# Running the experts of a transformer layer over two halves of the tokens, with the first half's rows fetched and combined beside the second half's tiles

## The reference, cut to what matters

```python
x = x + ga * attention(layernorm(x) * (1 + ca) + sa)
h = layernorm(x) * (1 + cb) + sb
probs = softmax(h @ gate_w.T + gate_b)
_, topi = top_k(probs, 2)
for e in range(8):
    y = relu(h @ w1[e] + b1[e])
    y = relu(y @ w2[e] + b2[e])
    y = y @ w3[e] + b3[e]
    out = out + cw[..., e:e + 1] * y      # cw: the token's probability of expert e if e is one of its two, else 0
x = x + gb * out
```

## Time and profile before

| | before |
|---|---|
| median of 3 runs | 3917.32 us (3915.02 to 3924.01) |
| the profiled execution | 3909.84 us |
| its span, first to last instruction | 3908.2 us |
| TensorE busy | 3369.7 us (86% of the span) |
| VectorE busy | 2338.5 us (60%) |
| ScalarE busy | 1389.0 us (36%) |
| GpSimd busy | 1262.1 us (32%) |

### The profile page before, as it was taken

One profiled execution on the slowest core, in us unless ns is written; L12 is line 12 of the kernel. 1 busy time (PEld: TensorE's weight loads), 2 busy tenths in 40 slices (PEclk: granted clock), 3 DMA queues, 4 the chain that ended last, 5 costly groups with the idle time before them and its releaser, 6 DMA issues. The chain is left out here.

```text
span 3908.2 us, 163045 instructions
## 1 busy us (share of the span) xinstructions
PE 3369.7 (86%) x72200; PEld 2918.7 (75%) x72200; DVE 2338.5 (60%) x4708; ACT 1389.0 (36%) x1655; POOL 1262.1 (32%) x1486
## 2 busy tenths in 40 slices
PE   6964999999989999999799999989999999399900
PEld 4534888888878888888788888878888887388800
DVE  5853566677256667753566777346677771466633
ACT  1320233344612334354123334522233446255511
POOL 1004432322354332233443322344333211222266
PEclk8986999999989999999899999999999999699955
DMA  3764101000321110003111000131000000544444
GB/s 111 208 165 117 36 24 34 29 27 19 86 60 39 32 37 26 19 29 106 39 39 37 29 19 26 44 95 39 29 29 29 22 13 11 179 141 144 137 129 140
DMA packets 241113, 251.41 MB, mean 64 GB/s; under 512 B 102808, under 2 KB 183676, under 8 KB 240300
## 3 DMA queue, kind: packets, MB, share of 16 engines
q1 hardware_dynamic: 219308, 197.69, 17.3%
q0 software_dynamic: 21120, 43.42, 3.6%
HBM read 149.52 MB, written 90.23 MB: 61 GB/s over the span
## 5 line engine op out<-in xcount | busy, mean ns | idle before, releaser
L884 DVE TENSOR_TENSOR att_acc<-att_pm,att_acc 128x512 f32<-128x512 f32 x1920 | 1267.1, 687 | 539.0 <-PE att_pm L1002 267.8
L963 ACT ACTIVATE att_pt<-att_ps 128x1024 f32<-128x1024 f32 x560 | 573.3, 1024 | 1615.2 <-PE att_ps L994 1606.7
L991 PE MATMUL att_ps<-att_qx,table_x 68*128 68x64 f16 x8960 | 734.0, 195 | 9.1 <-issue 9.0
L994 PE MATMUL att_ps<-att_qz,table_z 128*128 128x64 f16 x8960 | 733.0, 195 | 6.0 <-issue 5.9
L966 ACT ACTIVATE att_pt<-att_ps 128x1024 f32<-128x1024 f32 x528 | 515.1, 1022 | 346.7 <-PE att_ps L1002 344.6
L994 PEld LDWEIGHTS att_ps<-att_qz,table_z 128*128 128x128 f16 x8960 | 624.2, 99 | 10.9 <-issue 10.8
L991 PEld LDWEIGHTS att_ps<-att_qx,table_x 68*128 68x128 f16 x8960 | 621.3, 99 | 7.3 <-issue 6.8
L1084 PE MATMUL att_po<-att_pt,att_vn 128*32 128x128 f32 x17408 | 597.4, 278 | 2.4 <-issue 2.2
L987 PE MATMUL att_ps<-att_qs,att_kn 113*128 113x64 f16 x8960 | 456.8, 195 | 81.6 <-DMA att_qs<-s_m 75.8
L987 PE MATMUL att_pm<-att_qs,att_kn 113*128 113x64 f16 x8672 | 444.1, 195 | 83.8 <-POOL att_qx L757 49.5
L1084 PEld LDWEIGHTS att_po<-att_pt,att_vn 128*32 128x32 f32 x17408 | 448.5, 110 | 87.4 <-issue 73.0
(11 more groups left out here) (210 smaller groups left out, 3925.1 us busy)
## 6 DMA issues: line engine op xcount, KB each, us to landing
att_qe<-s_q SPq DMA_DIRECT2D x256, 128.0 KB
moe_xs<-s_h SPq DMA_DIRECT2D x71, 256.0 KB, 3.2
s_y<-moe_y SPq DMA_DIRECT2D x71, 256.0 KB, 2.2
s_v<-prj_vx SPq DMA_DIRECT2D x32, 512.0 KB, 3.9
att_vn<-s_v SPq DMA_DIRECT2D x64, 256.0 KB, 3.2
att_qs<-s_q SPq DMA_DIRECT2D x128, 66.0 KB
prj_x<-in_x POOLq DMA_DIRECT2D x16, 512.0 KB, 4.6
att_kn<-s_k SPq DMA_DIRECT2D x128, 64.0 KB, 2.4
```

The costliest lines, as they stand in the source:

```text
L884: dve.tensor_tensor(held, got, held, ALU.max).then_inc(bank_done, 1)
L963: act.activation(pt[:, k % 2, :, t * 64:t * 64 + 64].rearrange("p h (x c) -> p x h c", x=2), ps[t][:, :, :].rearrange("p x (h c) -> p x h ...
L991: last = pe.matmul(groups[:, :, g], keep["table_x"][:, y:y + P], qx[0:G * D + G, s, x * (XQ // G) + g], start=False, stop=(g == XQ // G - ...
L994: last = pe.matmul(groups[:, :, g], keep["table_z"][:, y:y + P], qz[:, s, x * (XQ // G) + g], start=False, stop=(g == XQ // G - 1), skip_g ...
```

## The change

`HALVES` = 2: the first 32 blocks of 128 tokens (two sequences) are half 0, the others half 1. Each half has regions of its own in `s_h` (`PART` rows a half), a `taken` of its own, zeros of its own, and tables of its own of `NH` = 2 * 4096 / 256 + 7 = 39 tiles, so `NT` is 78. Results go to `s_y0` and `s_y1`. `tables(f)` holds the former table work and `way_back(f)` the former L1303 to L1312 for 32 blocks. `tables(0)` runs ahead of the loop; `way_back(0)` runs on VectorE at the end of turn 8; `tables(1)` and `way_back(1)` at the end of turn 12. From turn `FETCH` = 43 on, GpSimd issues the two fetches of one block of half 0 behind its subtraction in each of 32 turns; ScalarE's and VectorE's share of that block comes two turns later at the end of their turns (`LAG` = 2), its store on SP two turns after that. The fetch buffers are 8 of one block in place of 2 of four blocks. After the loop come the 32 blocks of half 1 in the same manner, one by one.

```diff
-REGION = B * S + TL
+HALVES = 2
+REGION = B * S // HALVES + TL
+PART = NX * REGION + (NX - 1) * TL
...
-    NT = 2 * ROWS // TL + NX - 1
+    NH = 2 * ROWS // TL + NX - 1
+    NT, HB = HALVES * NH, NBLK // HALVES
...
+    FETCH, LAG = NH + 4, 2
...
@@ SP
-                for n in range(NX - 1):
-                    sp.dma_start(io["s_h"][DUMMY + n * TL:DUMMY + (n + 1) * TL]...
-                sp.wait_ge(tab_done, 1)
-                for e in range(NX):
-                    end = sp.value_load(tab_z[0:1, e:e + 1], min_val=0, max_val=NX * REGION)
+                for f in range(HALVES):
+                    for n in range(NX - 1):
+                        start = f * PART + DUMMY + n * TL
+                        sp.dma_start(io["s_h"][start:start + TL]...
+                sp.wait_ge(ends_done, 1)
+                for n in range(HALVES * NX):
+                    end = sp.value_load(tab_z[0:1, n:n + 1], min_val=0, max_val=HALVES * PART - TL)
                     sp.dma_start(io["s_h"][bass.ds(end, TL)]...
-                sp.wait_ge(zero_out, (2 * NX - 1) * 16)
+                sp.wait_ge(zero_out, HALVES * (2 * NX - 1) * 16)
+                sp.wait_ge(tab_done, 1)
...
                 for t in range(NT + 1):
...
+                    if 0 <= t - FETCH - LAG - 2 < HB:
+                        send(t - FETCH - LAG - 2)
+                for n in range(HB, NBLK):
+                    send(n)
@@ GpSimd
+                def fetch(n):
+                    if n % HB == 0:
+                        tiles_out = (n // HB + 1) * NH
+                        pool.wait_ge(back_done, n // HB + 1)
+                        for s in range(2):
+                            pool.wait_ge(y_out[s], (tiles_out + 1 - s) // 2 * 16)
+                    if n >= SLOTS:
+                        pool.wait_ge(summed, n - SLOTS + 1)
+                    for k in range(2):
+                        pool.indirect_dma_start(got[:, n % SLOTS, k, :], None, io[f"s_y{n // HB}"][:, :],
+                                                bass.IndirectOffsetOnAxis(ap=back[:, n, k:k + 1], axis=0)).then_inc(got_in[n % SLOTS], 16)
                 for t in range(NT):
...
                     pool.tensor_tensor(h1_s[:, t % 2, 1], h1_f[:, t % 2], h1_s[:, t % 2, 0], ALU.subtract).then_inc(h1_done, 1)
+                    if 0 <= t - FETCH < HB:
+                        fetch(t - FETCH)
+                for n in range(HB, NBLK):
+                    fetch(n)
@@ VectorE
+                def combine(n):
+                    s = n % SLOTS
+                    dve.wait_ge(first_done, n + 1)
+                    if n >= 4:
+                        dve.wait_ge(out_done, n - 3)
+                    dve.scalar_tensor_tensor(out=h[:, n % 4, :], in0=got[:, s, 1, :], scalar=keep["probs"][:, n, 1:2],
+                                             in1=got[:, s, 0, :], op0=ALU.mult, op1=ALU.add).then_inc(summed, 1)
+                    dve.wait_ge(summed, n + 1)
+                    dve.tensor_tensor(h[:, n % 4, :], h[:, n % 4, :], keep["gates"][:, 1, n // NB, :], ALU.mult).then_inc(gated, 1)
+                    dve.wait_ge(gated, n + 1)
+                    if n % JT == 0:
+                        dve.wait_ge(x_in[n // JT], 16)
+                    dve.tensor_tensor(x[:, n], h[:, n % 4, :], x[:, n], ALU.add).then_inc(out_done, 1)
+                tables(0)
...
+                    for f in range(HALVES):
+                        if t == NX + 4 * f:
+                            if f:
+                                tables(f)
+                            way_back(f)
+                    if 0 <= t - FETCH - LAG < HB:
+                        combine(t - FETCH - LAG)
+                for n in range(HB, NBLK):
+                    combine(n)
@@ ScalarE
+                def first(n):
+                    s = n % SLOTS
+                    act.wait_ge(got_in[s], (n // SLOTS + 1) * 2 * 16)
+                    act.activation(got[:, s, 0, :], got[:, s, 0, :], ACT.Copy, scale=keep["probs"][:, n, 0:1]).then_inc(first_done, 1)
...
+                    if 0 <= t - FETCH - LAG < HB:
+                        first(t - FETCH - LAG)
+                for n in range(HB, NBLK):
+                    first(n)
```

178 lines of the change are left out of this document (81 added, 97 removed).

## The result

| | before | after |
|---|---|---|
| median | 3917.14 us (20 runs, 3908.30 to 3924.01) | 3910.80 us (20 runs, 3906.75 to 3918.91) |
| ratio | 1 | 0.9987 (0.9981 to 0.9993) |
| profiled execution, span | 3908.2 us | 3911.5 us |
| TensorE idle before the first transposes | 47.96 us | 65.15 us |
| first to last turn's transposes | 320.3 us (70 turns on) | 387.4 us (77 turns on) |

The ratio puts the change 5 us ahead, 0.13%, which lies within the 0.2% that the prediction called no change; 27.6 us were forecast. The stages say where the rest is. They also hold one thing that the change hardly touches: in the profiled execution of after, TensorE ends its work in the attention 4.5 us later (3342.78 against 3338.29); the code there is the same but for the counters of the rows' places. Without it the stages add up to 17.2 + 67.1 - 85.5 = -1.2 us.

A forecast was written before the change was run, and what follows sets the result against it. TensorE was taken to bound the loop, and the issue of 128 GpSimd fetches the stretch behind it; overlapping them summed to -27.6 us, from a median of 3917.32 to 3889.7 us, range 3873 to 3914.

The forecast's parts named there:

- rival 1: Turns with a block: GpSimd's fetches stand still beside VectorE and set the pace, 3924 us, the same as before; chance 0.08.
- Fewer fetches: Behind the loop: 64 of 128 fetches move into the loop, at 1.307 us each, -83.6 us.
- Seven more tiles: Loop: 78 tiles in place of 71, each at 4.57 us, +32.0 us.
- Zeros: Before the first tile: SP writes 30 stretches of zeros in place of 15, +14.7 us, range +12 to +19.
- Table work: Two loop turns made late by table work on VectorE, 3.6 and 9.9 us, plus 2.7 for the clock: +16.2 us.
- which I add once, for the long stall: Table work in the loop: the low clock after idle time costs 2.7 us, counted for one of two late turns.
- The 32 turns: Loop turns with a block: TensorE keeps the pace of 4.57 us; +2 us for stretched instructions.
- It fits by 0.15 us: VectorE in a turn with a block: the added work needs 2.24 us from the start of L1297, and 2.39 are there.
- Start of the fetches: Behind the loop: the first fetch waits only for the last tile's store and starts at 3725.2, -3.1 us.
- Last block: End of the kernel: one block in place of four, 7.8 us after the last fetch's start instead of 13.6, -5.8 us.
- VectorE behind GpSimd: Turns with a block: VectorE waits for running fetches, about 4004 us, milder forms 3926 to 3939; chance 0.06 in all.
- The fifth: Rival: zeros at the pace of their writing and delays of 0.3 us a turn, +4 and +8, 3902 us; chance 0.12.

The follow-up runs named there:

- run 5: The change, with the second half's 15 stretches of zeros written one per turn from turn 8; 3844.78 us (0.9922) and 3844.38 us (0.9937).
- run 6: The change, with `way_back(0)`, `tables(1)` and `way_back(1)` moved ahead of the loop, 3887.28 us (0.9929); the unaltered change beside it, 3910.63 us (0.9990).
- Run 4: The change, with SyncE holding back each output store until VectorE is past its register load, in turns with a block; 3920.13 us, ratio 1.0013.
- run 1: The change, with VectorE's register load moved to mid-turn, where it would wait for ScalarE; 3842.88 us (0.9918) and 3895.01 us (0.9961).
- run 3: The change, with the loop's GpSimd fetches replaced by plain SyncE transfers of the same bytes from consecutive rows; 3848.65 us in one execution.
- run 9: The change with register load in mid-turn, second half's zeros beside the tiles and table work ahead of the loop; 3858.50 us (0.9860) and 3806.44 us (0.9832).

## Why the prediction was wrong

The mechanism was right in the main: each term is there, and none is new in kind but one. But the forecast of a gain clear of the noise failed. The sizes of four terms were low, all to the same side, and only the first term came out a little better. That the range held the time is luck: its upper part had been drawn toward rival 1, which did not come, and the forecast's own range of 3880 to 3899 missed.

- *Fewer fetches*, -83.6: right. The pitch fell to 1.28 us, which makes the term about 1.6 us better.
- *Seven more tiles*, +32.0: right, 4.57 us in nearly every turn with neither table work nor block.
- *Zeros*, +14.7: 17.2, of which run 5 shows 15.7 to be the stretches. The term took 0.75 us for a plain one; fourteen in a row take 1.00 each, which is 8.6 us more than seven and not 5.3. The upper end of 19 held it.
- *Table work*, +16.2: 20.9, and run 6 gives 19.4 back. The order and the place were right. Of the 4.7 us that were missing, 2.8 are idle time: 5.00 and 11.29 us in place of 3.6 and 9.9. The work itself took 5.8 and 12.2 us where 4.7 and 10.95 were forecast (one of its additions 1.06 us and not 0.23), and the exposed register load 0.9 each time and not 0.7. The other 1.9 are the clock, by the step "which I add once, for the long stall": the short stall, idle for 5.00 us, lost it too, and its layers took 2.74 and 2.77 us.
- *The 32 turns*, +2: 14.2. This is the step that failed. "It fits by 0.15 us" rested on 0.65 us for the register load with all that stands between it and L1342, and both parts of that were too small. Behind the load 0.54 us pass until L1342 starts, of which the 0.65 left 0.35; so even a load of 0.30 us makes 2.42 us from L1358, and 2.39 are there. The reserve was never there, though that alone would have cost 1 us in all. The load itself was put at 0.30 us, the median of the earlier trace rows, at a moment that the change moves: it now starts 2.0 us later against SyncE's store, meets its first packets, and takes 0.54 to 0.89 us in all but one turn. The maximum in the earlier trace rows, 552 ns, was a warning, though not the same meeting: it is the first load of all, at 3394.8, ahead of every store, while SyncE issued loads of a tile and of weights. Run 4 shows the meeting, run 1 the price: 11 to 15 us in these turns. The prediction's own sign of being wrong came true: a tile of 4.8 us or more in the second half, with VectorE as the releaser of TensorE (between 3645 and 3743 it ends ten waits of the first layer, 6.0 us).
- *Start of the fetches*, -3.1: -2.6; the first comes 2.99 us after the end of the last L1358, where 2.5 was forecast.
- *Last block*, -5.8: +2.0. In the short sessions exactly the forecast 7.8 us lie behind the last fetch (7.7 to 8.0 in eight profiles), in the long ones 15.2 to 18.1 with the change's form of the tail. The working was right for the instructions that it lists. That three short ones a block in place of seven instructions for four blocks would start late can't be read from any row of before.

Of the rivals, the first two (GpSimd as the pace, VectorE behind GpSimd) were looked for in the right stretch, with VectorE before TensorE as the releaser; runs 1 and 3 show that neither is the cause (in run 9 some fetches in the loop do take up to 1.47 us, and the turns do not follow them). The fifth, small delays of 0.3 us a turn with the zeros' upper end, 3902 us, was the nearest in kind; the delay was 0.5. What remains between -1.2 us of the stages and -5 us of the ratio is inside what two profiled executions of one kernel differ by: those of before have 569.9 and 574.0 us from TensorE's last work in the attention to the end of the span, those of the change 568.7 and 571.8.

Open is what delays VectorE's waits in the long sessions. Shown: late starts need the change's form of the tail (the kernel before has none in such a session), they grow with VectorE's instructions a block at 1.40 us each, they fall on steps of 0.70 us, they hit only instructions that wait for VectorE's own result in the same block, and two blocks an instruction remove them. What sets the 0.70 us, why they begin 33 to 73 us into the tail, why the loop, with more such instructions, has none, and whether the recording of the trace has a part in it, no run tells. Open too is what makes a session short or long: the kernel before has no profile from a short one, and the change itself was timed in none.

## What to carry to other kernels

Where a step is to fit into an engine's idle time with 0.15 us to spare, the chain behind it must be added up from rows in which it is not hidden, and a register load in it must be priced at its maximum, not its median. Moving the load to a place where the engine waits anyway is an edit of three lines. Work that is only needed for the second half of a loop (zeros, tables) should be looked for in every place that the change touches: the zeros and tables given here to the start and to two turns cost 38 us of a gain of 85, and 35 of them came back by a move of a few lines each. Before a late instruction is blamed on its neighbour, run the kernel in a second session: here some 8 us of the tail came and went with the session.

## What the runs showed of the hardware

- A register load from a table in the SBUF takes 0.30 us, also in the middle of a transfer at a DMA share of 1.0 (the kernel before, 3670.66 to 3670.97), and 0.58 where it meets the first packets of SyncE's store; with GpSimd's fetches as well, 0.82. It starts as the instruction in front of it starts, and L1342 starts 0.54 us after its end, so that behind an instruction of 0.42 us it shows at its full length.
- TensorE's granted clock fell to 0.50, the lower level, after an idle of 5.00 us: the next layers took 2.74 and 2.77 us, against 1.50 and 1.47.
- Fourteen writes of 256 KB of zeros from SyncE took 14.01 us, 1.00 each, where seven took 5.40, 0.77 each.
- A fetch of GpSimd behind the loop costs 1.26 to 1.29 us beside VectorE's instructions of 0.42, 1.32 beside 0.69, and 1.33 to 1.35 beside 1.22. That is the direction in which the Trainium skill's rule on the shared port points (page SBUF — State Buffer, section Who interferes with whom), at 0.05 us a fetch and not a whole instruction.
- In long sessions an instruction of VectorE that waits for VectorE's own result in the same block came 0.2 to 4.0 us late in the tail, on steps of 0.70 us, two of them for each instruction of a block.
